# One region for attention and dense layers: three chunks through ELU on GpSimd in the last rounds, the dense layers of two chunks interleaved

## The reference

```python
Wh = jnp.einsum('nf,hfd->hnd', x, W)                 # 8 heads of 64
e = jax.nn.leaky_relu(e_src[:, :, None] + e_dst[:, None, :], 0.2)
e = jnp.where(adj[None] > 0, e, NEG)
att = jax.nn.softmax(e, axis=-1)
h = jnp.einsum('hnm,hmd->hnd', att, Wh)
h = jax.nn.elu(h)
enc = jnp.transpose(h, (1, 0, 2)).reshape(x.shape[0], -1)
out = jax.nn.relu(enc @ W1.T + b1)                   # 512 -> 256
out = jax.nn.relu(out @ W2.T + b2)                   # 256 -> 128
out = jax.nn.relu(out @ W3.T + b3)                   # 128 -> 256
out = out @ W4.T + b4                                # 256 -> 512
...
x = x + out
```

## Time and profile before

| what | us |
|---|---|
| median of 3 runs | 982.78 (980.93 to 983.69) |
| time of the profiled execution | 983.48 |
| its span, first to last instruction | 981.7 |
| TensorE busy in the span | 867.9 (88%) |
| VectorE busy | 732.6 (75%) |
| ScalarE busy | 387.2 (39%) |
| GpSimd busy | 315.5 (32%) |

### The profile page before, as it was taken

How to read it: one execution, slowest core, us unless ns; L and a number is a source line. 1 busy time by engine, 2 the same in 40 slices (tenths; PEclk the granted TensorE clock), 3 DMA queues, 4 the chain that set the end, 5 groups by cost and what they waited for, 6 DMA issues and landing times. The chain is left out here.

```text
span 981.7 us, 16813 instructions
## 1 busy us (share of the span) xinstructions
PE 867.9 (88%) x5140; PEld 756.0 (77%) x5140; DVE 732.6 (75%) x1208; ACT 387.2 (39%) x698; POOL 315.5 (32%) x295
## 2 busy tenths in 40 slices
PE   1577889997999999989379999999999999948993
PEld 1466668886788888768279999999999999945551
DVE  5999992227555866666798999999999999966761
ACT  2511111211212121235266666666666666624330
POOL 1323343440000000047435555555555534300000
PEclk9799999998999999999779999999999999988998
DMA  9999520004723232040150000000000000012231
GB/s 332 407 312 299 190 86 0 0 0 159 206 87 105 87 106 86 1 170 0 36 199 23 22 21 23 23 21 21 27 27 22 22 21 22 0 54 97 86 129 46
DMA packets 36296, 87.70 MB, mean 89 GB/s; under 512 B 7056, under 2 KB 7952, under 8 KB 36240
## 3 DMA queue, kind: packets, MB, share of 16 engines
q1 hardware_dynamic: 35216, 82.98, 25.1%
q0 software_dynamic: 1040, 4.26, 1.2%
HBM read 74.45 MB, written 12.78 MB: 89 GB/s over the span
## 5 line engine op out<-in xcount | busy, mean ns | idle before, releaser
L930 DVE SCALAR_TENSOR_TENSOR l_q<-bank,l_neg_d,mask 128x512 fp32r<-128x512 f32 x512 | 338.6, 742 | 30.3 <-PE bank L1091 30.3
L1091 PE MATMUL bank<-l_parts,l_q 128*128 128x260 f32 x2048 | 250.8, 284 | 13.5 <-DVE l_q L930 13.5
L1091 PEld LDWEIGHTS bank<-l_parts,l_q 128*128 128x128 f32 x2048 | 248.8, 190 | 13.8 <-issue 11.7
L73 PE MATMUL bank<-l_x_hi,l_s_hi 128*128 128x512 f32 x256 | 102.7, 401 | 49.4 <-DVE l_x_lo L244 48.9
L961 ACT ACTIVATE l_mask<-mask 128x512 fp32r (+1 forms) x256 | 136.5, 619 | 0.7 <-PE bank L1111 0.5
L1111 PE MATMUL bank<-l_parts,l_mask 128*128 128x260 f32 x1024 | 129.6, 287 | 0.0
L1111 PEld LDWEIGHTS bank<-l_parts,l_mask 128*128 128x128 f32 x1024 | 128.1, 191 | 0.0
L73 PE MATMUL bank<-l_g_hi,l_a_hi 128*128 128x512 f32 x256 | 101.1, 395 | 6.2 <-DVE l_a_lo L609 5.9
L593 POOL TENSOR_TENSOR l_prod<-wh,l_a 128x512 f32<-128x512 f32 x32 | 37.5, 1195 | 214.4 <-ACT wh L572 206.7
L74 PE MATMUL bank<-l_x_lo,l_s_hi 128*128 128x512 f32 x256 | 101.1, 395 | 0.0
L75 PE MATMUL bank<-l_x_hi,l_s_lo 128*128 128x512 f32 x256 | 101.0, 394 | 0.0
(11 more groups left out here) (151 smaller groups left out, 1178.8 us busy)
## 6 DMA issues: line engine op xcount, KB each, us to landing
rows<-adj_t SPq DMA_DIRECT2D x48, 512.0 KB, 3.9
l_sum_a<-adj SPq DMA_DIRECT2D x16, 512.0 KB, 6.5
l_rows_b<-adj_t SPq DMA_DIRECT2D x16, 512.0 KB, 7.2
l_sum_b<-adj SPq DMA_DIRECT2D x16, 512.0 KB, 8.7
l_src<-e_rows SPq DMA_DIRECT2D x32, 256.0 KB, 3.1
wh_store<-wh POOLq DMA_DIRECT2D x1, 4160.0 KB, 14.0
l_h<-x SPq DMA_DIRECT2D x4, 1024.0 KB, 13.0
x<-x SPq DMA_DIRECT2D x1, 4096.0 KB, 15.0
```

The costliest lines, as they stand in the source:

```text
L73: pe.matmul(acc, hi, rhs_hi, start=first, stop=False, skip_group_check=True)
L930: v.scalar_tensor_tensor(out=q[:, i, :], in0=bank[S_BANKS[hh]][:], scalar=neg_d[:, i, h:h + 1], in1=mask[:, i, cols], op0=ALU.is_ge, op1=A ...
L1091: return pe.matmul(bank[Q_BANKS[hh][t]][:, 0:PW], q[:, i, t * P:(t + 1) * P], parts[:, pair_slot, hh, i, :], start=i == 0, stop=i == T - 1)
```

## The change

Attention and dense layers become one region (`attend_and_finish`), and the fallback hangs on one jump at its end. The last four rounds are written out instead of looped. The buffers of the dense layers take the places of attention buffers that are no longer used (`one_place`), so some of them can be filled while attention runs; `neg[1]` lies in the place of `w1_s`. In detail:

- SyncE loads the weights and the residual of chunk 0 in round 12, between the source rows.
- VectorE makes the shares of chunk c after its choices of round 13 + c (c = 0, 1, 2). GpSimd then averages chunk c and makes the parts of ELU (`average_chunk`, six operations) ahead of its `first_head` of that round, and adds them up (`elu_early`) behind it. ScalarE takes the exponentials between `take_m_sums(r)` and the casts for round r+1.
- Chunk 0 is transposed inside q(15,1). Chunk 3 has its ELU on VectorE during the dense layers (`elu_chunk`), by tiles.
- TensorE interleaves: the first layer of chunk c+1 stands between layers 1 and 3 of chunk c, and the transposes of chunk c+2 ahead of the last layer of chunk c.
- GpSimd adds the last bias to the residual (`add_bias`), which VectorE did.

```diff
-                    rounds(sp, hp, load)
+                    if hp + 1 < H // 2:
+                        rounds(sp, hp, load)
+                def load_last(r, k, b):
+                    load(r, k, b)
+                    if (k, b) == (0, 0):
+                        sp.wait_ge(q_done, T + 2 * T * (LAST - 3))
+                        sp.wait_ge(m_done, T + T * (LAST - 3))
+                        for dst, src_w in ((w1_s, w1_t.rearrange("(k p) f -> p k f", p=P)),
+                                           (b1_s, b1), (b2_s, b2), (b3_s, b3),
+                                           (w2_s, w2_t.rearrange("(k p) f -> p k f", p=P)),
+                                           (w3_s, w3_t), (w4_s, w4_t.rearrange("(k p) f -> p k f", p=P))):
+                            sp.dma_start(dst[:], src_w).then_inc(w_loaded, 16)
+                        sp.dma_start(b4_s[:, 0, :], b4.rearrange("(o f) -> o f", o=1).to_broadcast([P, F])
+                                     ).then_inc(w_loaded, 16)
+                        dense.load(sp, 0, x1_store)
+                last_rounds(load_last)
+                sp.wait_ge(q_done, T + 2 * T * (LAST + 1))
+                dense.load(sp, 1, x1_store)
+                for c in range(CHUNKS):
...
-                    rounds(v, hp, choose)
+                    if hp + 1 < H // 2:
+                        rounds(v, hp, choose)
+                def choose_last(r, k, b):
+                    choose(r, k, b)
+                    c = 2 * k + b - 1
+                    if c >= 0:
+                        v.wait_ge(summed, STEPS * (r + 1))
+                        dense.shares(v, c, 1, fine, retry_chain)
+                last_rounds(choose_last)
...
+                dense.take_lo(v, 0)
                 v.wait_ge(summed, STEPS * (LAST + 1))
-                for head in combine(v, LAST, slice(T - GT, T), H // 2 - 1):
-                    head()
+                first_head()
...
+                v.wait_ge(retry_chain, CHUNKS + 1)
+                v.tensor_reduce(fine_sum[:], fine[:].rearrange("p n o -> p (n o)"), AX_X, ALU.add
+                                ).then_inc(retry_chain, 1)
+                dense.elu_chunk(v, EARLY)
+                for c in range(CHUNKS):
...
+                        if not more and r == LAST - 3:
+                            a.wait_ge(w_loaded, 16 * 8)
+                            a.activation(w1_hi[:], w1_s[:], ACT.Copy).then_inc(w1_hi_ready, 1)
+                        if not more and r > LAST - 3:
+                            dense.exp_chunk(a, r - (LAST - 2))
+                        if not more and r == LAST:
+                            dense.take_hi(a, 0)
                         if more or r < LAST:
                             take_mask(r + 1, 0, after)
                             take_mask(r + 1, 1, after)
...
+                        last_rounds(serve)
+                dense.relu1(a, 0, 0)
+                dense.take_hi(a, 1)
+                dense.relu1(a, 0, 1)
+                for c in range(CHUNKS):
+                    if c + 1 < CHUNKS:
+                        dense.relu1(a, c + 1, 0)
+                    dense.relu2(a, c)
+                    if c + 1 < CHUNKS:
+                        dense.relu1(a, c + 1, 1)
+                    for m in range(K3):
+                        dense.relu3(a, c, m)
+                    if c == 0:
+                        for i in range(GT * EARLY, T):
+                            dense.exp_tile(a, i)
+                    if c + 2 < CHUNKS:
+                        dense.take_hi(a, c + 2)
...
+                        if not more and r > LAST - 3:
+                            dense.average_chunk(p, r - (LAST - 2))
                         first_head()
+                        if not more and r > LAST - 3:
+                            dense.elu_early(p, r - (LAST - 2))
...
                         for n in range(3):
                             cut_and_combine(4 * hp + n, n // 2, n % 2)
+                            if n == 0:
+                                p.wait_ge(w1_hi_ready, 1)
+                                p.tensor_tensor(w1_lo[:], w1_s[:], w1_hi[:].bitcast(F32), ALU.subtract
+                                                ).then_inc(w1_lo_ready, 1)
+                                p.wait_ge(w1_lo_ready, 1)
+                                dense.add_bias(p, 0)
+                dense.average_chunk(p, EARLY - 1)
+                dense.elu_early(p, EARLY - 1)
+                for c in range(1, CHUNKS):
+                    dense.add_bias(p, c)
...
+                    if i >= 8:
+                        if i == 8:
+                            pe.wait_ge(m_bank_free, GT * (LAST + 2))
+                        dense.turn(pe, 0, i - 8)
+                def dense_layers(of):
+                    of.sum1(pe, 0, 0)
+                    for k in range(KC):
+                        of.turn(pe, 1, k)
+                    of.sum1(pe, 0, 1)
+                    for c in range(CHUNKS - 1):
+                        of.sum1(pe, c + 1, 0)
+                        of.sum2(pe, c)
+                        of.sum1(pe, c + 1, 1)
+                        if of is dense and c == CHUNKS - 2:
+                            pe.wait_ge(retry_chain, CHUNKS + 2)
+                            pe.matmul(bank[of.TURN_BANKS[1]][0:1, 0:1], fine_sum[:], ones[:], start=True, stop=True
+                                      ).then_inc(fine_counted, 1)
+                        of.sum3(pe, c)
+                        if c + 2 < CHUNKS:
+                            for k in range(KC):
+                                of.turn(pe, c + 2, k)
+                        for t in range(GT - 1):
+                            of.sum_row(pe, c, t)
+                        if c == CHUNKS - 2:
+                            of.sum2(pe, c + 1)
+                        of.sum_row(pe, c, GT - 1)
+                    of.sum3(pe, CHUNKS - 1)
+                    for t in range(GT):
+                        of.sum_row(pe, CHUNKS - 1, t)
...
+                def sum_up_last(r, k, b):
+                    sum_up(r, H // 2 - 1, turn_first if r == LAST else None)
+                last_rounds(sum_up_last)
...
+                pe.wait_ge(q_bank_free, GT * (2 * LAST + 3))
+                dense_layers(dense)
...
+    def average_tile(self, v, i):
...
+        v.tensor_tensor(z, z, self.share[:, i * H:(i + 1) * H, :].to_broadcast([P, H, HD]), ALU.mult
+                        ).then_inc(self.last_averaged, 1)
+        v.wait_ge(self.last_averaged, j + 1)
...
+        v.tensor_scalar(self.last_neg[:, j % 2, :, :], z, 0.0, None, ALU.min).then_inc(self.last_neg_ready, 1)
...
+    def elu_chunk(self, v, c):
+        tiles = range(self.GT * c, self.GT * (c + 1))
+        for i in tiles:
+            self.average_tile(v, i)
+            if i > tiles[0]:
+                self.elu_tile(v, i - 1)
+        self.elu_tile(v, tiles[-1])
...
+    def add_bias(self, p, c):
...
+        p.wait_ge(self.x_loaded[c % 2], 16 * (c // 2) + 16)
+        p.tensor_tensor(res[:], res[:], self.b4_s[:].to_broadcast([P, self.GT, F]), ALU.add).then_inc(self.biased, 1)
...
+    def average_chunk(self, p, c):
+        n = self.GT * H // 2
+        p.wait_ge(self.share_ready, 2 * c + 2)
+        for k, z in enumerate(self.halves(c)):
+            share = self.share[:, (2 * c + k) * n:(2 * c + k + 1) * n, :]
+            p.tensor_tensor(z, z, share.to_broadcast([P, n, HD]), ALU.mult).then_inc(self.averaged, 1)
+            p.wait_ge(self.averaged, 2 * c + k + 1)
+            if c:
+                p.wait_ge(self.enc_ready, 2 * c - 1 + k)
+            p.tensor_scalar(self.neg[k], z, 0.0, None, ALU.min).then_inc(self.neg_ready, 1)
+        for k, z in enumerate(self.halves(c)):
+            p.wait_ge(self.neg_ready, 2 * c + k + 1)
+            p.tensor_scalar(z, z, 0.0, -1.0, ALU.max, ALU.add).then_inc(self.pos_ready, 1)
+    def elu_early(self, p, c):
+        for k in range(2):
+            i = self.GT * c + 2 * k
...
+            p.wait_ge(self.exp_ready, 2 * c + k + 1)
+            p.wait_ge(self.pos_ready, 2 * c + k + 1)
+            p.tensor_tensor(enc, z, neg, ALU.add).then_inc(self.enc_ready, 1)
...
+    def exp_chunk(self, a, c):
+        for k in range(2):
+            a.wait_ge(self.neg_ready, 2 * c + k + 1)
+            a.activation(self.neg[k], self.neg[k], ACT.Exp).then_inc(self.exp_ready, 1)
...
+    def turn(self, pe, c, k):
+        if c < self.early:
...
+        if KC * c + k >= 2:
+            pe.wait_ge(self.lo_ready, KC * c + k - 1)
...
+        for t in range(self.GT):
+            mm = pe.transpose(self.bank[self.TURN_BANKS[k % 2]][:, t * P:(t + 1) * P],
+                              self.packed[:, self.GT * c + t, k * P:(k + 1) * P], self.ident[:])
+        mm.then_inc(self.turned, 1)
```

More of the change, by code:

```diff
@@ L763, in _, with one_place, attend_and_finish @@
                           ).then_inc(top_spread, 1)
-def attend(nc, bank, wh, e, mask, e_rows, dst_top, wh_store):
+def one_place(nc, ctx, *groups):
+    made = []
```

(33 more changed lines are left out.)

755 lines of the change are left out of this document (372 added, 383 removed).

## The result

| what | before | after |
|---|---|---|
| median of the runs | 982.25 (980.93 to 983.69) | 996.64 (991.72 to 1001.0) |
| ratio, 95% interval | | 1.0141 (1.0116 to 1.0167) |
| profiled execution, span | 983.48, 981.7 | 1001.0, 999.2 |

The kernel became 1.4% slower. The four times of the changed kernel fall into two groups, 1000 to 1001 and 992 to 993; experiment 7 is about them. The profile shown is one of the upper group.

A forecast was written before the change was run, and what follows sets the result against it. It took TensorE, busy 88% of 981.7 us, as the bound. Terms summed to -8.2 us: 983.48 to 975.3, then 974.6 for the median, 0.7 lower; range 963 to 984 (the forecast's own 969 to 980).

The forecast's parts named there:

- A: Round 12: the source row for round 13 lands late behind the weight and residual loads; TensorE stalls 4.6 us (1.6 to 7.7).
- B: Start of round 14: ScalarE's exponentials wait for GpSimd's minima, one-input operations taken at 1.3 us; 4.6 us lost (3.4 to 7.9).
- C: Round 15: the same wait makes ScalarE's loop 26.1 us against a round of 23.2; adds 2.9 us (1.5 to 6.5).
- D: From attention to dense layers: the first layer starts 3.4 us after the last attention phase would have ended, not 19.1: -15.7 us.
- E: Dense layers: 68.3 us of pure work plus waits, 78.7 from first to last product against 77.9: +0.8 us.
- F: TensorE's half clock behind its new pauses, mostly swallowed in attention by ScalarE's loop: +3 us (0 to 9).
- G: Kernel end: about 4.4 us from the last row, against 12.8, TensorE's jump beside the store: -8.4 us (-6 to -9.5).
- GpSimd's other work hides: Round 15: combination, ELU sums and last averaging operations, 16 us, finish before the m-sum copies by some 2 us.
- Rival 3: GpSimd's one-input operations are slow: 982.8 us in all at 2.65 us each, about 990 at 3.5; chance 13%.
- Rival 1: Everything in attention hides, so its stalls and the clock cost are nothing: 959.5 us in all; chance 7%.
- Rival 2: The source row for round 13 lands in time, its stall 0 to 1 us, the rest stays: 970 us; chance 18%.
- Rival 4: Half clock behind each pause in full, 9 us, with the late source row at its upper bound: 984 us; chance 10%.

The follow-up runs named there:

- experiment 7: The changed kernel run again, unaltered: 999.07 us (991.69 to 1002.01), ratio 1.0155 to the kernel before.
- experiment 4: Changed kernel with SyncE's weight and residual loads issued behind the source rows of both heads of round 13: 989.48 us, ratio 1.0079.
- experiment 2: Changed kernel with GpSimd's one-input ELU operations moved to ScalarE, GpSimd subtracting the 1 with a two-input operation: 975.39 us, ratio 0.993.
- experiment 5: Changed kernel with ScalarE taking chunk 3's four exponentials sooner in its dense loop, not behind chunk 0's third layer: 990.27 us, ratio 1.0062.
- experiment 3: Changed kernel with ScalarE's exponentials of chunks 0 and 1 behind the next source row instead of ahead of the casts: 997.56 us, ratio 1.0165.
- experiment 6: Changed kernel with GpSimd's bias additions of chunks 1 to 3 waiting for VectorE's low parts of chunk 1: 993.69 us, ratio 1.0108.
- experiment 10: Kernel of experiment 9 with ScalarE's ELU operations of chunks 0 and 1 behind the next source row instead of ahead of the casts: 961.49 us, ratio 0.9789.
- experiment 9: Changed kernel with the edits of experiment 2, experiment 4 and experiment 5, bias additions waiting for VectorE's ELU of chunk 3: 965.07 us, ratio 0.9814.

## Why the prediction was wrong, by its own steps

The terms, from the starts of the phases in both traces. The changed kernel comes to m(12) 0.25 us later than the kernel before; that and the terms ahead are taken off each difference:

| term | predicted | measured | how measured |
|---|---|---|---|
| A | +4.6 | +7.3 | q(13,1) at 824.6, was 817.0 |
| B | +4.6 | +8.4 | m(14) at 848.3, was 832.3 |
| C | +2.9 | +9.9 | m(15) at 881.4, was 855.5 |
| D | -15.7 | -9.8 | first dense product at 906.4, was 890.3 |
| E and F | +3.8 | +10.2 | first to last product 88.1, was 77.9 |
| G | -8.4 | -8.8 | last row to the end 4.0, was 12.8 |

With the 0.25 they sum to +17.5, the difference of the spans.

*B, C and D failed first on one number*, "I take 1.3, nearer to the middle". The middle was between 0.69, another engine's price, and GpSimd's dearest two-input row, 2.47; the true prices, 2.78 and 3.63, lie above both ends, and outside the 0.9 to 2 us beyond which the prediction called itself wrong. Put in place of 1.3, the 2.78 of the minima (and 1.90 for the averages) gives 7.4 for B, most of the 8.4, and 5.7 for C, not 9.9. A one-input operation was assumed to cost no more than a two-input one of its size. The Trainium skill (GPSIMD Engine Reference, Elementwise and Engine selection) says the same, roughly line rate, which would be 0.9 us. The traces here contradict it, for this minimum, this maximum with an addition, and 1024 float32 elements a partition.

*The worse failure is of structure*, in C's sentence "GpSimd's other work hides". By the prediction's own prices GpSimd had 3.94 + 2.6 for averages and minima, 2.6 for maxima, 9.1 for the combination and 4 for the sums, 22.2 us in a round of 23.2, and it cannot overlap the next round's: the averaging waits for VectorE's shares, and these for the combination's last step. That loop is longer than a round once the four one-input operations cost 1.55 us each; the range for C reached to 6.5 us only because it was made from ScalarE's loop. Worked out from the rows of after, 2 x 1.90 + 2 x 2.78 + 2 x 3.63 + 9.2 + 4.4 = 30.2 us, and 2 us of waits: the 32.3 between two rounds' averages (823.8, 856.1). ScalarE's loop at the same prices is 28.9, so GpSimd's is the bound.

*Rival 3* was the right mechanism with the wrong point. It set the turn at 2.65 us and 990 us at 3.5, by six operations in a row and no loop beyond GpSimd's 2 us of slack; at 2.78 us its formula gives 983.5. For a price that no row showed, 13% was too little.

*A* held in mechanism: the fill waits 5.67 us for its transfer and comes at 792.4 (791.5 forecast), and experiment 4 takes it away whole. The time of the fill is partly luck: the transfers ahead were issued by 783.4 and not 785.1, and the row took 8.9 us to land and not 6. Its pauses are 3.35 and 0.84 us, 4.2 together (4.6 forecast). The other 3.1 us are the clock's, 0.91 over the first window: TensorE is busy 34.2 us for what takes 31.1 in experiment 4. F had this share as "mostly swallowed". In experiment 7's profile of the same kernel the pauses are 3.06 and 1.32 us, the clock stays at the full level, and the window is 36.0 us, so between 4.9 and 7.3 us A depends on the clock.

*D* missed by 5.9 us: the two late minima hold the exponential until 897.9 and so the high parts of chunk 0. The pause is 4.80 us, where the forecast had 2.7 of lateness with 1.75 of transposes in it, so 0.95; that is 3.8 us. The other 2.1 are TensorE's busy time, 11.6 us at a clock of 0.80 and not 9.5; the same window in experiment 2 has 9.8 at the full clock.

*E* was right for chunk 2's pause (6.5 forecast, 5.96) and for its reason, by experiment 5. For chunk 1's third transpose it had 1.4 us, and 6.4 came. "Waits that I find by following the rows of each engine" took each engine's rows at the length that they have alone. The Trainium skill (SBUF — State Buffer, Who interferes with whom) has the rule that was missed: a VectorE operation with two SBUF inputs and a GpSimd operation that reads SBUF exclude each other for their whole length. The trace agrees, 4.48 us for one of 0.43; by that rule the 4.6 us addition had to be a rival. The kernel before has the hold once too: L1382 takes 1.79 us at 889.52, beside GpSimd's L1484, and 1.22 where it runs alone. Without the long hold the dense layers take 81.6 to 81.7 us from first to last product (experiments 3, 4 and 6), so it costs 6.4 of the 88.1, the half clock behind it included. That these 81.7 are E and F as forecast is luck. The work at the full clock is 70.9 us in experiment 10 and not 68.3, and the 18.18 us of one chunk in the earlier trace rows had said so; the waits together are 9.0 and not 10.2 (with which the sum of E is 78.5, not 78.7); half clock is 1.8 and not 3.

*F*: TensorE is busy 74.4 us in the dense layers, against 70.9 for the same work at the full clock in experiment 10, so half clock costs 3.5 us there; 3 was forecast for the whole kernel, and A's 3.1 and D's 1.8 come to it. In rounds 14 and 15 GpSimd's loop sets the time whatever the clock. *G* held.

Rivals 1 and 2, that the stalls hide or the row comes in time, are out by A to C. Rival 4's half clock came nearly whole, 3.1, 1.8 and 3.5 us of its 9, and doesn't decide: it set 984.

## What to carry over

Before work moves to an engine with little to do, add up its whole round, with the new operations at a price that a row of that engine and that kind of operation shows, and look for a loop of waits that keeps rounds from overlapping; if no row shows the price, the range has to reach past the price at which the engine becomes the bound. Then ask which operations of the neighbour run beside it, VectorE with GpSimd above all. When the times of a kernel fall into groups, compare group with group, and compare stretches of the profiles and not only spans. When moving a waiting instruction in a queue gains nothing and the pause turns up elsewhere, the order in the queue was not the cause.

## What the runs showed of the hardware

- GpSimd on 128 x 1024 float32: two inputs, one of them a broadcast, 1.90 us; two full inputs 2.21; one input with one ALU operation 2.78; with two, 3.63. Here the number of inputs does not set the price. ScalarE's activation of that size takes 1.06.
- VectorE's operations with two SBUF inputs are held behind a running two-input GpSimd operation and end 0.3 to 0.6 us after it, up to 4.84 us for one of 0.42. Those with one PSUM and one SBUF input are not, 0.69 us beside it. Beside the last 0.6 us of a one-input operation (L1647) L914 kept its 0.42 us; no trace has more of an overlap with that kind.
- From 780 us on, in all traces, each pause of TensorE of 3.35 us and more is followed by a stretch at half the clock; behind pauses of 1.9 to 2.7 us it comes in some executions and not in others (behind 2.71 us in experiment 2 and 2.48 in experiment 9, not behind 2.73 and 2.48 in experiment 10). So part of each gain comes behind the pause that was taken away, and kernels that differ by 2 or 3 us can owe it to this.
